# TensorE multiplies a constant mask by the identity in three waits of a sort

## The chip, the cores and the metric

The kernel runs on one core of one Trainium2 chip. The metric is the device time of one execution in microseconds. The kernel before takes 1694.79 us, the median of 3 runs from 1694.64 to 1695.75.

## What is computed

A hybrid block over 2 x 1024 rows of 512 values: sliding window attention, a mixture of experts, a Mamba-2 mixer, and the same mixture of experts again, each with a layer norm ahead of it and a residual added. The change touches the two mixtures of experts:

```python
    x = x + _L0_attn_a_ref(_layernorm(x, axis=-1), L0_attn_a_w_qkv, L0_attn_a_w_out)
    x = x + _L0_ffn_ref(_layernorm(x, axis=-1), L0_ffn_gate_w, L0_ffn_w1, L0_ffn_w2)
    x = x + _L0_attn_b_ref(_layernorm(x, axis=-1), ...)
    x = x + _L0_ffn_ref(_layernorm(x, axis=-1), L0_ffn_gate_w, L0_ffn_w1, L0_ffn_w2)

        # _L0_ffn_ref
        logits = jnp.einsum('th,eh->te', x, gate_w)
        probs = jax.nn.softmax(logits, axis=-1)
        topw, sel = jax.lax.top_k(probs, TOP_K)
        topw = topw / jnp.sum(topw, axis=-1, keepdims=True)
        combine = jnp.zeros((T, E), dtype=x.dtype).at[jnp.arange(T)[:, None], sel].add(topw)
        gate_up = jnp.einsum('th,eoh->eto', x, w1)
        g, u = jnp.split(gate_up, 2, axis=-1)
        act = jax.nn.silu(g) * u
        expert_out = jnp.einsum('eti,ehi->eth', act, w2)
        out = jnp.einsum('eth,te->th', expert_out, combine)
```

There are 8 experts, each row goes to 2 of them, and an expert has 352 inner values.

## The kernel before

The program is four stages one behind the other: `attention`, `experts` with the tag moe_a, `mamba`, `experts` with the tag moe_b. Each stage is a block with a program for each engine, written out by hand with semaphores; between stages all engines meet at a barrier.

The kernel does not compute all experts for all rows. It sorts the (row, expert) pairs by expert into 39 slots of 128 rows, gathers the rows of a slot by an indirect DMA, multiplies them by the weights of the slot's expert, and adds the results to the rows in memory by an indirect DMA. The weights of three experts fit into a ring in SBUF (`load_expert`, L912, 4352 KB an expert, issued by SyncE); the first expert's load is issued as the block begins.

`run_slots` (L1033) holds the block. Its first part is the sort, one for each mixture of experts, and the engines take turns in it:

- VectorE (`sort_rows`, L1173) chooses the experts of the last two tiles (the first fourteen are chosen during the stage before) and raises `both_ready` (L975).
- TensorE (`rank_last`, L1298 to L1310) waits for it and counts, in 17 small bf16 matmuls into bank 3, the rank of each row in its expert (first L1302).
- VectorE makes the start of each expert, each row's place, and from them, in four parts, two tables of 8 x 39 values each (L1202, L1204, L1206); each part raises `tables_ready`. Then it computes the owner of each slot (L1208, L1210).
- TensorE (`lists`, L1312 to L1320) waits for each part and makes 64 fp32 matmuls into bank 7, each with its own 128 columns of weights and 78 columns streamed (L1317): they bring each row's number and weight to its slot.
- VectorE waits for all of them, makes the indices (L1212, L1213) and the tables of which ring place and which load a slot needs (`slots_ready`).
- GpSimd gathers the rows of slots 0, 1, 2 and 3 (L1084); the gather of slot 2 and on waits for rows turned.
- TensorE waits for `slots_ready`, reads four values into registers (L1277, L1280), waits for the gather, and turns the rows of slot 0 by four transposes (`turn`, L1244) into bank 0. ScalarE and VectorE split them in a high and a rest part (L1110, L1164). TensorE then makes the up products (`up`, L1261), 24 matmuls for slot 0 in two halves of 12, each streaming 352 columns in fp32r, and turns slot 1.

Behind that runs the steady part, slot by slot: up products, the turn of the activations (L1272), the turn of the next rows, and down products (`down`, L1292, 9 matmuls of 512 columns, into banks 6 and 7 by turns). The down products of slot 0 are the first ones to write bank 6, with `start` set in the first matmul. The reads of registers for slot s+2 stand behind the first and the second pass of three down products of slot s.

The operands of the change are constants: `identb` (L137), the 128 x 128 identity in bf16, and `ssd_mask` (L142), 128 x 512 in bf16, zeros and -1e30, made before the first stage. In `mamba`, `running_sums` (L2092) multiplies the same two, twice in a call, as the start of an accumulation. Matmuls in a row: each weight load (PEld in the profile) overlaps the matmul ahead of it.

Of the kernel before, what the change touches and what calls it, by code (L numbers as in the profile page):

```python
# [97 lines left out]
def spread(ap, axis, n):  # L98

    v = ap.unsqueeze(axis)  # L100
    shape = list(v.shape)
    shape[axis] = n
    return v.broadcast_to(shape)
# [929 lines left out]
def run_slots(core, tag, sem, x_rows, xn_rows, index, weight, place, needed, ends, w_split, weights_in, in_w, at, sort):  # L1033

    nc, bank, arena = core.nc, core.bank, core.arena
# [25 lines left out]
    with nc.Block(no_gpsimd_drain=True) as block:  # L1061
# [176 lines left out]
        def _(pe):  # L1238
# [59 lines left out]
            def rank_last():  # L1298
                E, N = EXPERTS, sort.EARLY
                pe.wait_ge(both_ready, 1)  # L1300
                out = rank_bank[:, 0:3 * E]
                nc.tensor.matmul(out, core.before[:], sort.both[:, N:N + 3].rearrange("p t e -> p (t e)"),  # L1302
                                 start=True, stop=False)
                for t in range(N):
                    nc.tensor.matmul(out.rearrange("p (t e) -> p t e", e=E), core.onesb[:],
                                     spread(sort.both[:, t], 1, 3), start=False, stop=False)
                nc.tensor.matmul(rank_bank[:, E:3 * E].rearrange("p (t e) -> p t e", e=E), core.onesb[:],
                                 spread(sort.both[:, N], 1, 2), start=False, stop=False)
                nc.tensor.matmul(rank_bank[:, 2 * E:3 * E], core.onesb[:], sort.both[:, N + 1], start=False, stop=True)\
                    .then_inc(ranks_made, 1)  # L1310

            def lists():  # L1312
                n = TOPK * TILES
                for j in range(n):
                    if j % PART == 0:
                        pe.wait_ge(tables_ready, j // PART + 1)
                    last = nc.tensor.matmul(list_bank[:, 0:2 * SLOTS].rearrange("p (c s) -> p c s", c=2),  # L1317
                                            sort.at_spot[:, j // TILES, j % TILES], sort.by_slot[:, :, j],
                                            start=(j == 0), stop=(j == n - 1))
                last.then_inc(lists_made, 1)  # L1320

            rank_last()
            lists()
            places, needs = {}, {}

            def look_up(s, j):
# [965 lines left out]
```

## Time and profile before

| | us |
|---|---|
| median of 3 runs | 1694.79 |
| the profiled execution, its own time | 1690.24 |
| its span, first to last instruction | 1688.4 |
| TensorE busy (matmul) | 1516.6 |
| VectorE busy | 906.7 |
| ScalarE busy | 715.7 |
| GpSimd busy | 604.4 |
| mean granted TensorE clock, share of full | 0.957 |

All rows come from one execution taken by the hardware profiler. Times of day count from the first instruction. PE is TensorE's matmul, PEld its weight load, DVE VectorE, ACT ScalarE, POOL GpSimd, SP SyncE. A matmul's duration is longer than its distance to the next one in a row, since they are pipelined; the end of a group is the end of its last one. The granted clock is 1.00 at 2.4 GHz and 0.50 at 1.2 GHz.

### The profile page before, as it was taken

Reading aid. Unit: us, or ns where it says so; the run is one execution under the profiler, and the core shown is the slowest. Engines: PE = TensorE matmul, PEld = TensorE weight load, DVE = VectorE, ACT = ScalarE, POOL = GpSimd, SP = SyncE. Lnnn points to the kernel's source line nnn. Section 1 sums busy time; section 2 is a strip of 40 time slices with the busy share of each in tenths; the row PEclk is TensorE's granted clock in tenths of the full one; section 3 lists DMA queues with packets and bytes.
Section 4 is the critical chain, followed back from the end, with each engine's and each line's share of the span. In section 5 each row is a group of like instructions: output and inputs, shape, how many; then the busy total and the mean of one; then the engine's idle time right before and its main releaser. Section 6 shows DMA issues by size and latency. Waiting matters only on the chain. (4 is left out here: it accounts for less than half of the span.)

```text
span 1688.4 us, 33729 instructions
## 1 busy us (share of the span) xinstructions
PE 1516.6 (90%) x11806; PEld 1249.9 (74%) x11822; DVE 906.7 (54%) x2087; ACT 715.7 (42%) x1776; POOL 604.4 (36%) x469
## 2 busy tenths in 40 slices
PE   3999999998689999995899999999999868999997
PEld 3787887786578888985767677666776447888897
DVE  3676677776622224225687785877857652222222
ACT  2666666666122224322554455544445302222232
POOL 5564555555122334433232223322223302333342
PEclk9999999999689999997999999999999968999999
DMA  5264454454559777533010101101000136787643
GB/s 207 88 207 145 173 199 158 165 188 169 184 188 337 195 228 208 117 62 90 14 33 20 51 20 33 32 20 47 24 20 20 32 125 207 232 238 223 186 88 57
DMA packets 94476, 212.34 MB, mean 126 GB/s; under 512 B 7184, under 2 KB 7184, under 8 KB 92944
## 3 DMA queue, kind: packets, MB, share of 16 engines
q1 hardware_dynamic: 76736, 166.58, 28.2%
q0 software_dynamic: 17472, 40.90, 12.1%
q10 hardware_dynamic: 144, 3.15, 0.5%
q8 instruction: 85, 1.39, 0.3%
q14 instruction: 39, 0.32, 0.1%
HBM read 136.94 MB, written 73.66 MB: 125 GB/s over the span
## 5 line engine op out<-in xcount | busy, mean ns | idle before, releaser
L1261 PE MATMUL bank<-ring,halves 128*128 x1872 | 336.2, 329 | 3.5 <-ACT halves L1110 3.5
L1261 PEld LDWEIGHTS bank<-ring,halves 128*128 128x128 f32 x1872 | 307.0, 191 | 11.2 <-issue 4.8
L498 POOL TENSOR_TENSOR arena<-arena 128x1024 f32<-128x1024 f32 x64 | 123.9, 1936 | 146.6 <-DVE arena L574 145.0
L1655 DVE SCALAR_TENSOR_TENSOR arena<-arena 128x256 f32<-128x256 f32 x240 | 146.1, 651 | 18.6 <-ACT arena L1857 15.8
L1120 ACT ACTIVATE arena<-bank 128x512 f32<-128x512 f32 x78 | 46.7, 598 | 221.1 <-DMA out_dram<-arena 79.9
L700 ACT ACTIVATE arena<-arena 128x256 f32<-128x256 f32 x256 | 126.4, 500 | 1.1 <-DVE arena L566 1.1
L779 PE MATMUL bank<-arena 128*128 128x128 f32 x1024 | 124.9, 281 | 1.7 <-ACT arena L681 0.8
L1084 POOL DMA_INDIRECT arena<-normalised_rows,arena x78 | 80.3, 1030 | 125.1 <-DVE arena L1213 56.9
L779 PEld LDWEIGHTS bank<-arena 128*128 128x128 f32 x1024 | 118.9, 195 | 7.6 <-issue 2.6
L1546 POOL TENSOR_TENSOR arena<-arena 128x1024 f32<-128x1024 f32 x16 | 31.3, 1959 | 249.3 <-ACT arena L1908 227.9
L2107 PE MATMUL bank<-arena 128*128 128x512 f32 x256 | 117.0, 611 | 1.2 <-ACT arena L1901 1.2
L1092 POOL DMA_INDIRECT mid_rows<-arena x39 | 61.8, 1586 | 155.7 <-issue 107.9
L1092 POOL DMA_INDIRECT out_dram<-arena x39 | 61.8, 1585 | 152.2 <-issue 106.3
L1110 ACT ACTIVATE halves<-bank 128x512 fp32r<-128x512 f32 x78 | 46.7, 598 | 158.1 <-PE bank L1244 155.5
L1159 DVE TENSOR_TENSOR moe_b_act_rest<-bank,moe_b_act_high 128x384 fp32r<-128x384 f32 x39 | 21.8, 558 | 154.1 <-ACT moe_b_act_high L1125 149.9
L2022 PE MATMUL bank<-halves,w_in_high 128*128 128x256 f32 x640 | 94.8, 292 | 5.7 <-ACT arena L1857 4.3
L2107 PEld LDWEIGHTS bank<-arena 128*128 128x128 f32 x256 | 48.5, 194 | 68.7 <-issue 67.1
L1159 DVE TENSOR_TENSOR moe_a_act_rest<-bank,moe_a_act_high 128x384 fp32r<-128x384 f32 x39 | 21.7, 557 | 126.6 <-ACT moe_a_act_high L1125 126.6
L2022 PEld LDWEIGHTS bank<-halves,w_in_high 128*128 128x128 f32 x640 | 83.6, 194 | 7.4 <-ACT arena L1857 4.5
L1865 ACT ACTIVATE arena<-arena 128x256 f32<-128x256 f32 x80 | 35.6, 500 | 110.2 <-DVE arena L1655 110.1
L1164 DVE TENSOR_TENSOR halves<-bank,halves 128x512 fp32r<-128x512 f32 x78 | 53.9, 691 | 52.0 <-ACT halves L1110 52.0
L819 PE MATMUL bank<-ident,arena 128*128 128x128 f32 x512 | 70.0, 282 | 7.0 <-POOL arena L498 7.0
(263 smaller groups left out, 3184.0 us busy)
## 6 DMA issues: line engine op xcount, KB each, us to landing
ring<-expert_halves SPq DMA_DIRECT2D x16, 4352.0 KB
expert_halves<-expert_high SPq DMA_DIRECT2D x16, 1088.0 KB, 8.5
expert_halves<-expert_rest SPq DMA_DIRECT2D x16, 1088.0 KB, 10.7
arena<-in_w_dram SPq DMA_DIRECT2D x8, 1088.0 KB, 6.5
normalised_rows<-arena SPq DMA_DIRECT2D x33, 256.0 KB, 2.0
arena<-in_x_dram SPq DMA_DIRECT2D x32, 256.0 KB, 2.8
arena<-mid_rows SPq DMA_DIRECT2D x32, 256.0 KB, 2.8
w_in_raw<-in_in_w_dram SPq DMA_DIRECT2D x16, 290.0 KB
```

The source lines that it names most:

```text
L498: nc.gpsimd.tensor_tensor(held, held, spread(rinv[:, HG * g:HG * g + HG], 2, 2 * P), ALU.mult)\
L700: last = nc.scalar.activation(held, held, ACT.Exp, scale=-1.0, bias=nmax[:, h:h + 1], accum_out=psum_p[:, h:h + 1])
L779: last = nc.tensor.matmul(proj[:, c * P:c * P + P], wqkv[:, k, first + c * P:first + c * P + P], xnT[:, k], start=(k == 0), stop=(k == KD ...
L819: last = nc.tensor.transpose(b[:, j * P:j * P + P], probs[:, g // 2, HG * (g % 2) + 2 * half + j // 2, (j % 2) * P:(j % 2 + 1) * P], core. ...
L1084: nc.gpsimd.indirect_dma_start(out=rows[:, s % 2], out_offset=None, in_=xn_rows, in_offset=bass.IndirectOffsetOnAxis(ap=index[:, s:s + 1], ...
L1092: nc.gpsimd.indirect_dma_start(out=x_rows, out_offset=bass.IndirectOffsetOnAxis(ap=index[:, s:s + 1], axis=0), in_=y[:, s % 2], in_offset= ...
L1110: nc.scalar.activation(rows_parts[0][:, par], bank[0][:], ACT.Copy).then_inc(rows_high, 1)
L1164: nc.vector.tensor_tensor(rows_parts[1][:, par], bank[0][:], rows_parts[0][:, par], ALU.subtract)\
L1261: last = nc.tensor.matmul(bank[1 + 2 * par + part][:, 0:INTER], rows_parts[a][:, par, k * P:k * P + P], weights(at, b, (2 * k + part) * IN ...
L1655: last = nc.vector.scalar_tensor_tensor(out=slot[:, j], in0=cin[:, c, k:k + PAIR], scalar=taps[:, c, k:k + 1], in1=slot[:, j], op0=ALU.mul ...
L2022: last = nc.tensor.matmul(unit_banks[unit][:, j * PAIR:(j + 1) * PAIR], w_parts[b][:, k, at:at + P], x_parts[a][:, k], start=((a, b, k) == ...
L2107: last = nc.tensor.matmul(bank[7][:], yT[:, k], w_out[:, k], start=(k == 0), stop=(k == KY - 1))
```

## The change

A helper on TensorE makes n matmuls of the identity by the mask, each of 512 columns, into bank 6, each with `start` and `stop` set, so that it overwrites what stands there. It is called three times in each sort: with 3 ahead of the ranks, with 16 between the ranks and the lists, with 18 between the lists and the wait for `slots_ready`. Nothing reads the results, no semaphore is added, and nothing else is changed.

```diff
@@ -1319,8 +1319,17 @@
                 last.then_inc(lists_made, 1)
 
+            def stay_busy(n):
+
+                for _ in range(n):
+                    nc.tensor.matmul(bank[6][:], core.identb[:], core.ssd_mask[:].rearrange("p a b -> p (a b)"),
+                                     start=True, stop=True)
+
+            stay_busy(3)
             rank_last()
+            stay_busy(16)
             lists()
+            stay_busy(18)
             places, needs = {}, {}
```

## Rows read from the trace of the kernel before

**Rows 1.** The page: span, and granted clock in 40 slices, in tenths.

```profile
span 1688.4 us, 33729 instructions
...
PEclk9999999999689999997999999999999968999999
```

**Rows 2.** TensorE's waits in the first sort: total us, times, longest.

```profile
PE bank L1317 <- DVE arena L1206: 6.0, 1, 6.0
PE bank L1244 <- DMA arena<-normalised_rows,arena: 5.2, 1, 5.2
```

**Rows 3.** Windows: length, busy us of PE PEld DVE ACT POOL, clock, DMA share, GB/s.

```profile
449.30:455.20 5.90, 0.00 (x0) 0.00 (x0) 5.29 (x21) 0.00 (x0) 0.00 (x0) 0.50 1.04 394
...
462.50:465.90 3.40, 3.40 (x18) 3.40 (x17) 0.00 (x0) 0.00 (x0) 0.00 (x0) 0.50 0.00 0
...
471.50:474.30 2.80, 0.00 (x0) 0.00 (x0) 0.05 (x1) 0.00 (x0) 1.49 (x2) 0.50 0.42 108
...
476.30:479.50 3.20, 3.11 (x11) 3.11 (x12) 0.56 (x1) 0.00 (x0) 0.92 (x1) 0.50 0.29 82
479.70:482.40 2.70, 2.69 (x18) 2.44 (x17) 0.00 (x0) 0.00 (x0) 0.00 (x0) 1.00 0.00 0
```

**Rows 4.** Timeline, first sort: start us, us, what, count, idle before and releaser.

```profile
447.27 0.24 DVE L965 MAX8 arena<-logits 128x8 f32<-128x8 f32 x2 [1.11 <-PEq L118]
...
448.68 0.20 PE L1302 MATMUL bank<-arena,before 128*128 128x24 bf16 x1 [2.79 <-DVE arena L975]
...
455.29 13.73 PEld L1317 LDWEIGHTS bank<-arena 128*128 128x128 f32 x64 [6.08 <-DVE arena L1206]
455.29 13.94 PE L1317 MATMUL bank<-arena 128*128 128x78 f32 x64 [6.00 <-DVE arena L1206]
...
459.54 0.44 DVE L1210 TENSOR_REDUCE arena<-arena 128x39 f32<-128x273 f32 x1
...
474.38 1.12 PE L1244 MATMUL bank<-ident,arena 128*128 128x128 f32 x4 [5.15 <-DMA arena<-normalised_rows,arena]
...
476.39 5.57 PE L1261 MATMUL bank<-ring,halves 128*128 x24 [0.89 <-ACT halves L1110]
```

**Rows 5.** Timeline, second sort.

```profile
1381.67 13.94 PE L1317 MATMUL bank<-arena 128*128 128x78 f32 x64 [5.99 <-DVE arena L1206]
...
1402.61 6.57 PE L1261 MATMUL bank<-ring,halves 128*128 x24 [0.89 <-ACT halves L1110]
```

**Rows 6.** Timeline, the same kinds of work at full clock; the second row at half.

```profile
1351.34 0.97 PEld L230 LDWEIGHTS bank<-gate,arena 128*128 128x128 f32 x8 [0.92 <-ACT arena L224]
...
1370.38 1.71 PEld L230 LDWEIGHTS bank<-gate,arena 128*128 128x128 f32 x8 [0.92 <-ACT arena L224]
...
481.80 0.60 PE L1244 MATMUL bank<-ident,arena 128*128 128x128 f32 x4
...
492.62 2.17 PE L1261 MATMUL bank<-ring,halves 128*128 x12
```

**Rows 7.** Instructions of L2092, and of L844 from 435: ns min/median/max, first to last start.

```profile
L2092 PE MATMUL bank<-ssd_mask,identb x16: 377/379/379, 811.8 to 1329.8; 128*128 128x512 bf16 x16
...
L844 PE MATMUL bank<-wo_high,halves x7: 632/632/767, 435.4 to 438.1; 128*128 128x512 f32 x7
```

**Rows 8.** Windows in moe_a, two where TensorE waits, and what follows the first.

```profile
544.46:547.87 3.41, 1.41 (x8) 1.04 (x9) 1.13 (x3) 1.93 (x4) 1.59 (x1) 1.00 1.04 404
547.87:551.30 3.43, 3.43 (x10) 2.66 (x11) 0.61 (x1) 0.00 (x0) 0.99 (x1) 0.50 1.10 338
...
609.30:612.70 3.40, 1.67 (x12) 1.38 (x11) 0.00 (x0) 0.51 (x2) 0.00 (x0) 1.00 0.41 123
```

**Rows 9.** Reads of registers on TensorE's queue, and a down product.

```profile
L1277 PEldq TENSOR_LOAD <-arena x1: 302/302/302, 500.5 to 500.5; - x1
...
L1280 PEldq TENSOR_LOAD <-arena x2: 298/302/305, 471.6 to 472.9; - x2
...
501.71 1.66 PE L1292 MATMUL bank<-ring,moe_a_act_high 128*128 x6
```

## Prediction

> **What bounds the kernel now.** I read the page first: 1688.4 us of span, and a row of granted clock that stands at nine tenths nearly everywhere, with dips in two regions, around the eleventh and the thirty-third of the forty slices [rows 1]. These are the two places where a block of experts begins with its sort. The waits of TensorE there come next: it waits 6.0 us for VectorE's tables and 5.2 us for the gather of the first rows [rows 2]. The windows give the clock of each stretch: 0.50 in the wait for the tables, 0.50 in the middle of the list matmuls although TensorE is busy for all 3.40 us of 3.40, 0.50 in the wait for the gather, 0.50 in the first 3.2 us of the up products, and 1.00 only behind them [rows 3]. So in the sort TensorE works at 1.2 GHz, and the reader is to see that the 64 list matmuls do not lift the clock by themselves, though they run for 13.94 us on end [rows 4], while the up products do.
>
> The timeline gives the chain, which is the same in both sorts. VectorE starts at 447.27, TensorE has the ranks done at 455.29 - 6.00 = 449.29, VectorE makes tables, the list matmuls run from 455.29 to 469.23, VectorE turns them into indices, GpSimd issues the gather, it lands, TensorE turns the rows from 474.38 for 1.12 us, ScalarE copies, and the up products of the first slot run from 476.39 for 5.57 us [rows 4]. VectorE has nothing to do from about 460.0 (its last operation of the sort starts at 459.54 and takes 0.44) until the lists are done [rows 4]. So TensorE is the bound in the lists, the turn and the up products, and each microsecond there ends the program a microsecond earlier, as the experts behind the sort are started by these products; the loads of their weights are started by the rows turned and move along.
>
> **The change, part by part.** It removes nothing and moves nothing. It adds 3 + 16 + 18 matmuls of 512 bf16 columns per sort, 37 in each, 74 in all, that write a bank which the first down product starts afresh. They add no wait on a semaphore; what stands behind them on TensorE is the work that they precede.
>
> *Price of one.* The same operation, identity by mask, is in the mamba stage, where its matmul takes 379 ns [rows 7]. In a row the distance counts, not the duration: 512 columns at 2.4 GHz are 0.213 us, at 1.2 GHz 0.427 us. The trace doesn't show a row of bf16 ones; the nearest, 512 columns of fp32r at 0.50, has 7 starts between 435.4 and 438.1, 0.45 apart [rows 7]. I take 0.427 and keep 0.45 as the upper end.
>
> *First wait, 3 of them.* If TensorE enters the block with VectorE at 447.27, 3 x 0.427 = 1.28 plus about 0.1 for the first weight load (an estimate from the start) ends at 448.65, and the ranks start at 448.68 [rows 4]. Nothing to 0.15 late; I take 0.05.
>
> *Second wait, 16 of them.* They start at 449.29 and the lists may start at 455.29, so there are 6.00 us. All at 1.2 GHz they take 6.83, 0.83 too long. In the first sort dense products lift the clock 3.3 us after their start (476.39 to some point after 479.5) [rows 3, 4]; in the second they take 6.57 us instead of 5.57 [rows 5], so it came later: at full clock 12 of them take 2.17 [rows 6], 0.168 apart with 0.32 for the last (an estimate), at 1.2 GHz 352 columns make 0.293, and 6.57 us are then 19 of 23 distances at half rate, 5.6 us. If the clock rises x us after the start, the filler ends x + (6.83 - x)/2 after it: 5.07 for 3.3, 6.2 for 5.6. Nothing late in the one and 0.2 in the other; between the ends 0 and 0.83 I take 0.1, since the dense products are the nearest rows.
>
> *Lists at full clock.* Their distance is set by the weight load of 128 fp32 columns, since a load with hardly any columns behind it has the same: 8 loads before 8-column matmuls take 0.97 us at full clock and 1.71 where the clock has fallen [rows 6]. That is 0.121 and 0.214 for one, and the 64 loads of the lists in 13.73 us make 0.215 [rows 4]. At full clock a list matmul takes between half of that, 0.107, and 0.121, which has the long end of the last load in it; 64 take 6.9 to 7.7, I take 7.3: 6.6 less. VectorE keeps up: all four tables are done before 459.54 [rows 4], one every 1.3 us, and TensorE would take one in 16 x 0.11 = 1.8.
>
> *Third wait, 18 of them.* At full clock 18 x 0.213 = 3.84 us in a wait of 5.15 (469.23 to 474.38) [rows 4]: nothing, 1.3 us are left. At half rate 7.69: 2.5 late. Behind them stand four reads of registers which take 2.7 us from the moment when the slots are ready, so they must not wait for the filler: the last starts at 472.9 [rows 9]. In the steady loop such a read is made at 500.5, though in the code it stands behind the first three down products, which start at 501.71 [rows 9], so they run beside the filler. If they had to wait for its end they would be over 3.84 + 2.7 = 6.5 after the lists, 1.4 too late in each sort; I take 0.
>
> *Turn and up products.* Four transposes 1.12 to 0.60: 0.52 less [rows 4, 6]. 12 up products take 2.17 at full clock [rows 6], so 24 take 4.2 (the second dozen follows without a start of its own), against 5.57 and 6.57 [rows 4, 5]: 1.4 and 2.4 less.
>
> *Sum.* First sort: -6.6 - 0.52 - 1.4 + 0.05 + 0.1 = -8.37. Second: -9.37. Together -17.7 us. Nothing takes the cover away: the load of the first expert's weights runs beside the tables (no transfers in the window at 462.5) [rows 3], so a gather some 7 us earlier meets no traffic.
>
> A sentence of the Trainium skill speaks against the change: TensorE: Matmul & The Clock Gate, Why this matters for your kernels, says that keeping TensorE busy without a break brings it to the full clock. By that, lists of 13.94 busy us should run at full clock already and filling the waits would give at most the turn and the up products, some 5 us. The row says otherwise, 0.50 all along [rows 3], so I go by the row.
>
> **The rivals.** *Held only in part.* Once high, the clock must survive stretches that are half full: the gap that a quick filler leaves before the lists (0 to 0.9 us), the lists themselves (78 columns per 128 loaded), and the 1.3 us, turn and 0.9 us between the last filler and the up products. The trace shows both outcomes: a stretch of 3.4 us with TensorE busy for 1.67 kept 1.00, one with 1.41 busy was followed by 0.50 [rows 8]. The lists are busy throughout, so I think that they hold it; the last gap is the weak one. Falling there leaves 6.6 + 0.52 - 0.15 = 6.97 of one sort's gain; losing it in both gives -13.9, in one -15.3 or -16.3. If it falls inside the lists, about half of them are quick (3.3 us), the last filler is partly slow (about 1 late) and turn and up are quick: about -4.2 and -5.2 per sort, -9.4 for both and -13 or so for one.
>
> *Not counted, slower.* The filler multiplies an identity, nearly all zeros, by a mask of zeros and one large value, and no row here shows that such matmuls lift a clock; the only ones of the kind, pairs in mamba, stand in a stretch at full clock. If they don't count, every one costs 0.427: 0.1 + 0.83 + 2.54 = 3.5 per sort, +7.0. It turns slower from the point where the last filler, at 18 x the distance, exceeds 5.15 us, a distance of 0.286, with nothing won in the lists. Against it: the array streams 512 columns whatever they hold.
>
> The Trainium skill (TensorE: Matmul & The Clock Gate, Part 4: PE-mode transpose) says that transposes don't count as busy the way matmuls do; the filler has the identity as an operand, but isn't issued as a transpose, and if the rule reached it the time would be that of this rival.
>
> *It does not do what it says.* If only the up products profit (clock rising late, lists slow): -0.52 - 1.4 and -0.52 - 2.4, plus 0.83 and about 1 in each sort for late fillers: -1.2, which can't be told from no change.
>
> **How the numbers follow.** The profiled execution took 1690.24 us for its span of 1688.4; the median shown is 1694.79, 4.55 above. Taking 17.7 off gives 1672.5 for a profiled execution and 1677.1 for the median, which I predict. Its own range is -16 to -19.5. Chances: this 0.70; held in part 0.22 (-9 to -16.5); only turn and up 0.02; not counted 0.06 (+7.0, 1701.8). The range for 8 in 10 takes the forecast and most of the second: 1674.5 to 1683. What a measurement of this kernel can tell from no change is about 0.2%, 3.4 us. Faster by more: 0.92; within: 0.02; slower by more: 0.06.
>
> **What would show it.** In the changed profile the window over the lists reads 1.00 and they take 7.2 to 7.5 us; the wait before them is nearly gone; the turn takes 0.60; the 24 up products 4.0 to 4.3. Lists at 13.9 us with the filler 0.427 apart would show the slower rival; up products at 5.6 or more behind quick lists the gap after the last filler. A turn that starts more than 5.2 us after the lists would show that the fillers or the reads behind them are late. And if all of this is as written and the end is not 17 to 18 us earlier, something behind the sort, a transfer, took it back.

## Result

| | us |
|---|---|
| before, median of 4 runs (1694.64 to 1696.12) | 1695.27 |
| after, median of 4 runs (1677.29 to 1681.86) | 1679.55 |
| profiled execution: before / after | 1690.24 / 1681.86 |
| span: before / after | 1688.4 / 1680.1 |
| mean granted clock: before / after | 0.957 / 0.967 |

The ratio is 0.9907, 95% interval 0.9889 to 0.9925: 15.7 us quicker by the medians, where 17.7 were forecast. The two profiled executions differ by only 8.4 us; the stages below show where the rest lies in this pair.

The page of the changed kernel, lines that answer to [rows 1]; each dip at a sort was two slices at 6 and 8 tenths and is one at 7:

```profile
span 1680.1 us, 33893 instructions
...
PEclk9999999999799999997999999999999979999999
```

The windows of the changed kernel's first sort, which answer to [rows 3] (length, busy us of PE, PEld, DVE, ACT, POOL, clock, DMA share, GB/s):

```profile
449.40:452.40 3.00, 3.00 (x12) 1.07 (x9) 2.53 (x12) 0.00 (x0) 0.00 (x0) 0.50 0.98 382
452.50:454.40 1.90, 1.90 (x9) 0.69 (x7) 1.69 (x7) 0.00 (x0) 0.00 (x0) 1.00 1.05 396
454.60:455.40 0.80, 0.00 (x0) 0.00 (x0) 0.80 (x3) 0.00 (x0) 0.00 (x0) 1.00 1.06 392
455.60:459.00 3.40, 3.40 (x32) 3.40 (x32) 3.30 (x9) 0.00 (x0) 0.00 (x0) 1.00 1.06 390
...
466.10:469.50 3.40, 1.29 (x7) 0.52 (x5) 0.18 (x1) 0.60 (x1) 0.86 (x2) 1.00 0.56 154
469.60:472.90 3.30, 3.30 (x11) 3.30 (x12) 0.41 (x1) 0.00 (x0) 0.77 (x1) 0.50 0.29 79
```

The filler starts at half clock and has brought the full one about 3.1 us later; an idle gap of 0.99 us follows, the clock stays; in the lists TensorE is at 32 matmuls in 3.40 us where [rows 3] had 18. The last two windows are the gap behind the last filler: the clock is still 1.00 in it and 0.50 when the up products come. TensorE's timeline of both sorts, which answers to [rows 4] and [rows 5]:

```profile
447.46 1.44 PE L1325 MATMUL bank<-ssd_mask,identb 128*128 128x512 bf16 x3 [1.38 <-PEq L118]
448.87 0.20 PE L1302 MATMUL bank<-arena,before 128*128 128x24 bf16 x1
...
449.35 5.13 PE L1325 MATMUL bank<-ssd_mask,identb 128*128 128x512 bf16 x16
455.48 7.37 PE L1317 MATMUL bank<-arena 128*128 128x78 f32 x64 [0.99 <-DVE arena L1206]
462.68 4.05 PE L1325 MATMUL bank<-ssd_mask,identb 128*128 128x512 bf16 x18
468.00 0.66 PE L1244 MATMUL bank<-ident,arena 128*128 128x128 f32 x4 [1.27 <-DMA arena<-normalised_rows,arena]
469.55 5.63 PE L1261 MATMUL bank<-ring,halves 128*128 x24 [0.89 <-ACT halves L1110]
...
1374.82 4.91 PE L1325 MATMUL bank<-ssd_mask,identb 128*128 128x512 bf16 x16
1380.95 7.37 PE L1317 MATMUL bank<-arena 128*128 128x78 f32 x64 [1.23 <-DVE arena L1206]
1388.16 4.05 PE L1325 MATMUL bank<-ssd_mask,identb 128*128 128x512 bf16 x18
1393.28 0.66 PE L1244 MATMUL bank<-ident,arena 128*128 128x128 f32 x4 [1.08 <-DMA arena<-normalised_rows,arena]
1394.83 4.11 PE L1261 MATMUL bank<-ring,halves 128*128 x24 [0.89 <-ACT halves L1110]
```

In both sorts the lists take 7.37 us instead of 13.94 and nothing starts late. In the second the up products take 4.11 instead of 6.57; in the first they stay at 5.63 (before 5.57).

The profiled executions in six stretches, from the starts of the instructions named (of the up products that of their first weight load):

| from - to | before | after | difference |
|---|---|---|---|
| start - ranks of the first sort | 448.68 | 448.87 | +0.19 |
| ranks - up products of slot 1, first sort | 34.59 | 27.62 | -6.97 |
| to the last scatter of moe_a | 278.61 | 278.04 | -0.57 |
| mamba with the ends of the stages around it, to the ranks | 613.18 | 619.81 | +6.63 |
| ranks - up products of slot 1, second sort | 35.42 | 25.91 | -9.51 |
| to the last scatter of moe_b | 272.49 | 274.39 | +1.90 |

The two sorts bring 16.5 us. Mamba, in which not one instruction is changed, takes 6.6 us longer. That takes back two fifths of the 16.5 in this pair, and it is the first question to the experiments.

### The profile page after: what moved, and what is told of

It is laid out like the page before. It is cut to its first block and busy times, and to the rows that moved or that the text cites. A ratio compares the mean times of both kernels' runs of the same rounds, so it can differ in the third digit from the quotient of the medians.

```text
span 1680.1 us, 33893 instructions
## 1 busy us (share of the span) xinstructions
PE 1529.3 (91%) x11896; PEld 1246.7 (74%) x11896; DVE 908.3 (54%) x2087; ACT 716.3 (43%) x1776; POOL 601.9 (36%) x469
## 3 DMA queue, kind: packets, MB, share of 16 engines
q10 hardware_dynamic: 144, 3.15, 0.5%
```

## Experiments

"Ranks to up" is in all tables the time from the first rank matmul to the up products of slot 1 (before 34.59 and 35.42, after 27.62 and 25.91); "mamba" is the time from its first normalised tile to the ranks of the second sort (before 602.51, after 609.15). A version with one run has no interval.

### Delay alone ahead of mamba, and a second profile of the kernel before

At the end of moe_a's block, on VectorE, five memsets in the kernel before, one in the changed kernel (the line that declares the semaphore `padded` is left out):

```diff
+            if in_w is not None:
+                dve.wait_ge(added, 16 * SLOTS)
+                pad = Chain(dve, padded)
+                for _ in range(5):          # 1 in the changed kernel
+                    pad(nc.vector.memset(bank[5][:], 0.0))
```

> The kernel before with VectorE making five memsets of a free bank, one behind the other, at the end of the first experts' block, about 2.7 us of pure delay ahead of mamba. In the changed kernel mamba came 7.3 us earlier and took 6.6 us longer than before (from its start to the ranks of the second sort), and the clock fell for a short stretch in more of its turns. Theory (where mamba lies against the moments at which the clock is set decides which weak stretches lose it, and nothing else): a delay alone changes mamba's length too, by some us, with the clock falling at other turns than in the kernel before; a value of 3 to 6 us longer if it lands where the changed kernel does. Rival (the fillers themselves lengthen mamba, by something that lasts): mamba as long as before within 0.3 us and the clock falling at the same turns, total +2.7.

> The changed kernel with one such memset at the same place, about 0.6 us of delay. Theory: mamba's length moves again, by more than the delay; if it lands where the kernel before does, mamba is 5 to 6 us shorter than in the changed kernel's profile and the whole is 4 to 6 us quicker than that profile in spite of the delay. Rival (lasting effect of the fillers): mamba stays 6.6 us longer than before, total +0.6.

> The kernel before once more, for a second profile. Theory (mamba's length moves with the turns in which the clock falls, in the kernel before as well): mamba takes 604 to 610 us instead of 602.5 if the clock falls in more than the five turns of the first profile, and the stretches of the two sorts are the same (34.6 and 35.4 from the ranks to the up products of slot 1, the second one between 34.0 and 36.0). Rival (602.5 is what mamba takes in the kernel before, and the change lengthens it by 6 us): 602.5 within 0.5.

| | ranks to up | mamba | the whole, median |
|---|---|---|---|
| before, 5 memsets | 34.61, 35.36 | 607.20 | 1697.70 (10 runs), ratio 1.0019 [1.0002, 1.0037] |
| changed, 1 memset | 27.68, 25.83 | 608.81 | 1681.38 (6 runs), ratio 0.9919 [0.9893, 0.9944] |
| before, again | 34.52, 35.40 | 607.68 | 1691.51 (1 run) |

With five memsets and no filler in the kernel, mamba is 4.7 us longer than in the first profile of the kernel before; but the second profile of that kernel, unchanged, has it 5.2 us longer too. So no effect of the delay on mamba is shown, and the median with the delay, 3.4 us above the 1694.30 timed beside it, is little more than the memsets themselves (3.15 us from the first to the end of the last). The rival in its full size (the fillers lengthen mamba by 6.6 us) falls by the second profile. A small part of it doesn't: the three profiles without fillers have 602.5, 607.2 and 607.7, the eleven with fillers 607.3 to 612.1, 609.3 on average, so that 1 to 3 us that the change gives back in mamba stay possible. The windows of the second profile of the kernel before, over three stretches early in mamba's loop at half clock, and below them the same times of day in its first profile (mamba starts 2.9 us later there, so the work in them isn't quite the same; from 801.0 to 1083.7 us that profile is at 1.00 throughout):

```profile
871.30:874.70 3.40, 3.40 (x16) 3.24 (x15) 1.49 (x4) 1.99 (x5) 0.00 (x0) 0.54 0.00 0
...
943.00:946.30 3.30, 3.30 (x16) 3.16 (x15) 1.31 (x2) 1.75 (x5) 0.00 (x0) 0.53 0.00 0
1014.70:1018.00 3.30, 3.30 (x16) 3.22 (x15) 1.18 (x2) 1.61 (x5) 0.00 (x0) 0.54 0.00 0
```

```profile
871.30:874.70 3.40, 3.40 (x34) 3.31 (x34) 1.61 (x4) 2.73 (x6) 0.00 (x0) 1.00 0.00 0
943.00:946.30 3.30, 3.30 (x25) 3.05 (x24) 1.30 (x2) 2.68 (x7) 0.00 (x0) 1.00 0.00 0
1014.70:1018.00 3.30, 3.23 (x17) 2.40 (x16) 2.50 (x7) 2.78 (x7) 0.35 (x1) 1.00 0.03 5
```

In the 3.3 us ahead of each of the three TensorE is busy for 2.76, 2.71 and 2.71 us; such a stretch is called weak here. The second profile has eight short stretches at half clock in mamba's loop, the first one five. Three more and 5.2 us more make 1.7 us for each. The first profile of the kernel before, on which the forecast was worked out, had the shortest mamba of all 14 profiles. It doesn't explain why that execution lay 4.55 us under its median: the second one, with a mamba 5.2 us longer, took 1691.51 us, only 1.3 more, since its other stages were shorter, and lay 2.5 under the median timed beside it.

What was expected of the one memset was wrong: it did not bring the changed kernel's mamba back to 602.5; it took 608.8, the length that the rival had given. The falls follow each other 71.7 us apart in mamba's loop, save the last one, and the same part of the loop loses the clock in some executions and not in others. What decides it, and whether its place in time can move it, was not shown.

### One group of fillers at a time

```diff
 e_only16                e_no16                 e_no3
-stay_busy(3)            stay_busy(3)          -stay_busy(3)
 rank_last()             rank_last()            rank_last()
 stay_busy(16)          -stay_busy(16)          stay_busy(16)
 lists()                 lists()                lists()
-stay_busy(18)           stay_busy(18)          stay_busy(18)
```

> The changed kernel with only the 16 matmuls between the ranks and the lists; those ahead of the ranks and those behind the lists are left out. Theory (the clock is what the lists lack, and the 16 bring it): lists about 7.4 us in both sorts as in the changed kernel, but in the wait behind them the clock falls, so the turn takes 1.1 us and the 24 up products 5.6 to 6.6: 6.5 us gained per sort, 13 at the two places against the kernel before. Rival (the three groups work only together, the clock falls in the lists): lists at 13.9 us or between, nothing gained.

> The changed kernel without the 16; the 3 and the 18 stay. Theory: lists at half clock, 13.9 us; the 18 behind them start slow, need 3.3 to 5.6 us to bring the clock and end 5.5 to 6.6 us after the lists, so the turn comes 0.3 to 1.5 us later than before after the lists' end, but turn (0.6) and up products (4.1) are quick: gain of 0.5 to 2.5 us per sort. Rival (matmuls of the mask don't count, something else quickened the lists): the 18 take 7.7 us and the turn comes 2.5 late, up products slow.

> The changed kernel without the 3 matmuls ahead of the ranks. Theory (the 3 only fill; the 16 are enough since they need 3.3 us or a bit more of dense work): lists in 7.4 us in both sorts, ranks up to 0.1 us earlier, the 16 up to 0.5 us longer than the 4.9 to 5.1 they took. Rival (the 3 are needed to bring the clock in time): the 16 take over 6.2 us and the lists start late, or part of them runs at half clock.

| | lists | lists' end to turn | up products x24 | ranks to up |
|---|---|---|---|---|
| only the 16 | 7.37, 7.37 | 5.19, 4.97 | 5.50, 6.48 | 27.99, 28.74 |
| without the 16 | 13.94, 13.94 | 5.61, 5.25 | 4.10, 4.10 | 33.06, 32.69 |
| without the 3 | 7.37, 7.37 | 5.12, 5.00 | 5.61, 4.11 | 27.57, 25.98 |

TensorE's timeline, first sort with only the 16 (one record of the fillers is missing), then without them:

```profile
456.61 7.37 PE L1317 MATMUL bank<-arena 128*128 128x78 f32 x64 [0.91 <-DVE arena L1206]
469.17 1.12 PE L1244 MATMUL bank<-ident,arena 128*128 128x128 f32 x4 [5.19 <-DMA arena<-normalised_rows,arena]
471.17 5.50 PE L1261 MATMUL bank<-ring,halves 128*128 x24 [0.89 <-ACT halves L1110]
```

```profile
455.94 13.94 PE L1317 MATMUL bank<-arena 128*128 128x78 f32 x64 [5.99 <-DVE arena L1206]
470.10 5.56 PE L1325 MATMUL bank<-ssd_mask,identb 128*128 128x512 bf16 x17 [0.22 <-issue]
475.49 0.60 PE L1244 MATMUL bank<-ident,arena 128*128 128x128 f32 x4
```

The parts are nearly as expected (without the 16, the turn of the second sort comes 5.25 us after the lists instead of 5.5 or more, and the gain there is 2.7 us instead of at most 2.5). The 16 bring 6.6 and 6.7 us, nearly all of it in the lists. The 18 keep the clock over the wait for the gather: 0.4 of 7.0 us in the first sort, where the clock is lost a moment later anyway, and 2.8 of 9.5 in the second. Without the 16, the 18 (with the 3) bring 1.5 and 2.7 us, although they start at half clock and the turn comes 0.3 to 0.5 us late. The 3 bring nothing: ranks to up is 27.57 and 25.98 without them, 27.62 and 25.91 with them. The single run without them took 1674.3 us, which looked like a further gain of 5 us; so it was timed again.

> The changed kernel without the 3 once more, timed. Theory (the 3 bring nothing and carry the risk of the early rise): lists of 7.4 us in both sorts again, the median of the whole within 2 us of the change's, on either side, as the dips in mamba decide. Rival (the 1674.3 of the single run show a gain of 5 us from leaving the 3 away): a median of 1673 to 1676.

Median 1680.85 (4 runs), ratio 0.9918 [0.9898, 0.9938], lists 7.37 in both sorts, ranks to up 27.64 and 25.80. The 1674.3 came from short stretches elsewhere (mamba 607.6, experts of moe_b 270.7; in the second 612.1 and 274.3).

### What is streamed

```diff
-                for _ in range(n):
-                    nc.tensor.matmul(bank[6][:], core.identb[:], core.ssd_mask[:].rearrange("p a b -> p (a b)"),
-                                     start=True, stop=True)
+                for _ in range(2 * n):
+                    nc.tensor.transpose(bank[6][:, 0:P], core.ones[:], core.ident[:])
```

> The changed kernel with each of the fillers replaced by two transposes of 128 x 128 fp32 (ones against the identity), so 6, 32 and 36 of them; each is 0.213 us at half clock and 0.109 at full, as in the turn of the rows, so the time filled is the same. Theory (what keeps the clock up is that the array is streamed through, by what operation does not matter): lists in 7.4 us, as in the changed kernel. Rival (transposes don't count for the clock): lists at 13.9 us, the last 36 take 7.7 us, the turn comes 2.5 us late, and the kernel is some 6 us slower than before.

First sort: lists 7.37, ranks to up 27.69. These transposes do for the clock what the mask does there. The profile lists them as MATMUL of 128 x 128 fp32, as it does the turns of rows, and doesn't say in which mode the engine ran them. The second sort was not as expected:

```profile
1368.94 4.41 PE L1325 MATMUL bank<-ident,ones 128*128 128x128 f32 x32
1375.08 11.97 PE L1317 MATMUL bank<-arena 128*128 128x78 f32 x64 [1.72 <-DVE arena L1206]
1386.84 6.09 PE L1325 MATMUL bank<-ident,ones 128*128 128x128 f32 x36
1393.27 0.65 PE L1244 MATMUL bank<-ident,arena 128*128 128x128 f32 x4 [0.33 <-issue]
```

The 32 ended after 4.41 us instead of 5.2, left 1.72 us idle, and the lists took 11.97. The next experiment had the same.

### Bridging the last gap

```diff
             lists()
-            stay_busy(18)
+            stay_busy(23)
...
             turn(0)
+            stay_busy(4)
             pe.wait_ge(weights_in, needs[0])
```

> The changed kernel with 23 matmuls behind the lists instead of 18 and 4 more between the turn of slot 0's rows and the up products. Theory (in the first sort the clock falls in the gap between the last filler and the up products, and only there): the clock stays at 1.00 there, the 24 up products take 4.1 instead of 5.6 us in the first sort, the second sort is as in the changed kernel; the turn comes 5.2 us after the lists and the up products 1.54 us after it, or at most 0.2 later. From the ranks to the up products of slot 1: 26.1 in the first sort (changed kernel 27.6), 25.9 in the second; 1.5 us quicker in all, hardly more than the noise of the whole. Rival (the clock falls at a set place of the program whatever fills the gap): 5.6 us again and the total unchanged or later by what the 9 matmuls cost.

Beside it the changed kernel once more:

> The changed kernel once more, beside the version with the bridged gap. Theory: the same stretches in both sorts within 0.1 us (27.6 us from the ranks to the up products of slot 1 in the first sort), while mamba and the experts behind the sorts differ by some us from the profile seen, because the clock falls in other turns. Rival (mamba's 609 us are a fixed consequence of the change): 609.1 within 0.3 us.

| | lists | up products x24, first sort | ranks to up | mamba | the whole, median |
|---|---|---|---|---|---|
| bridged | 7.37, 12.01 | 4.12 | 26.11, 32.25 | 608.36 | 1678.03 (5 runs), 0.9900 [0.9882, 0.9918] |
| change again | 7.37, 7.37 | 5.66 | 27.73, 25.97 | 608.92 | 1679.81 (4 runs), 0.9921 [0.9906, 0.9937] |

The expectation for the change again was in part wrong: the sorts repeat within about 0.1 us, but mamba did not move by some us. It took 608.92, within the 0.3 that the rival gave around 609.15. So the changed kernel has 609.15 and 608.92, and 608.81 with the memset, and the 1 to 3 us from above stay open.

In the first sort the bridge does what it should: the gap is filled, the clock holds, and the 24 up products take 4.12 us. So the fall there is made by the thin stretch from the last filler to the up products. In the second sort the clock fell in the lists. Windows of the bridged version: the gap before the lists, the first 2.2 us of the lists, the rest, the filler behind them:

```profile
1377.20:1378.90 1.70, 0.00 (x0) 0.00 (x0) 1.60 (x6) 0.00 (x0) 0.00 (x0) 1.00 1.04 394
1379.00:1381.20 2.20, 2.20 (x20) 2.20 (x20) 2.13 (x6) 0.00 (x0) 0.00 (x0) 0.98 1.05 392
1381.30:1390.70 9.40, 9.40 (x46) 9.40 (x46) 2.27 (x6) 0.00 (x0) 0.00 (x0) 0.50 0.31 115
1390.80:1394.80 4.00, 4.00 (x11) 1.48 (x10) 1.88 (x10) 0.00 (x0) 2.04 (x2) 0.50 0.14 17
```

There the 16 had taken 4.31 us, since the clock came early, and 1.81 us stayed idle. Two explanations offered themselves: such a gap makes the clock fall a little later, in the lists, or the fall is chance. The 3 fillers ahead of the ranks can be the reason for the early clock, since they begin the dense work 2 us sooner. Two more runs, 12 instead of 16 in the changed kernel, and the bridged version without the 3:

```diff
 e_12                    e_no3_bridge
 stay_busy(3)           -stay_busy(3)
 rank_last()             rank_last()
-stay_busy(16)           stay_busy(16)
+stay_busy(12)           lists()
 lists()                 stay_busy(23)   # and 4 behind turn(0)
```

> The changed kernel with 12 fillers ahead of the lists instead of 16, the 3 and the 18 as they are. Theory (an idle gap of nearly 2 us or more before the lists, with the lists behind it, makes the clock fall): the 12 end 4.0 to 4.4 us after their start, the gap is 1.7 to 2.1 us, and in at least one of the sorts the clock falls in the lists, which then take 9 to 12.5 us. Rival (the lists hold any clock that they are given at their start): 7.4 us in both sorts, the gap is harmless.

> No filler ahead of the ranks, 16 ahead of the lists, 23 behind them, 4 between the turn and the up products. Theory (with the 3, the clock can rise early, the 16 then end 1.7 us or more before the lists, and the clock falls in the lists, as in the second sort of the version with the bridged gap and of that with transposes; without the 3 it can't rise before about 3 us of the 16 are done): lists 7.4 us in both sorts, the gap before them under 1.3 us, the up products of slot 0 in 4.1 us in both, from the ranks to the up products of slot 1 26.0 to 26.1 and 25.8 to 26.0. In all 1.5 us quicker than the change and the best of all versions, if only by the noise. Rival (the early fall in the lists was chance and the 3 have nothing to do with it): lists of 12 us may come up again in one of the sorts.

With 12 the lists took 13.73 and 13.94 us, as if there were no filler, more than the 9 to 12.5 expected. Windows of the gap and of the lists in both sorts:

```profile
451.90:454.20 2.30, 0.39 (x3) 0.09 (x1) 2.13 (x8) 0.00 (x0) 0.00 (x0) 1.00 1.05 395
454.30:467.50 13.20, 13.20 (x64) 13.20 (x64) 4.36 (x11) 0.00 (x0) 0.00 (x0) 0.50 0.40 146
1384.20:1386.00 1.80, 0.01 (x1) 0.00 (x0) 1.66 (x6) 0.00 (x0) 0.00 (x0) 1.00 1.04 390
1386.40:1400.00 13.60, 13.60 (x64) 13.60 (x65) 4.46 (x11) 0.00 (x0) 0.00 (x0) 0.50 0.40 147
```

The clock is 1.00 while TensorE is idle and 0.50 once it works. In a longer wait it falls within the wait: with only the 16, behind the lists of the first sort, TensorE is idle from 463.98 to 469.17, and the clock is 1.00 in 464.10:467.40 and 0.50 in 467.50:469.10. Gaps of 1.92 and 2.10 us made the lists slow here, 1.72 and 1.81 in the two versions above. All shorter ones were harmless, in the other sorts of all versions with 16 fillers, up to 1.51 in the second sort of the change again and 1.69 in that of the changed kernel with the memset. In this version only the filler was shortened, by the 4 that would have filled the gap, so the gap is the cause of its two falls. In the two versions above the same is likely, from four falls in four longer gaps and none below. A fixed limit isn't shown: 1.69 and 1.72 lie too near each other, and the fall came 2.2 us into the lists in those two versions and within 0.3 us of their start here, so where the gap lies in time may count as well as how long it is. The kernel took 1691.27 us (1 run).

Without the 3 and with the bridge: lists 7.37 in both, gaps of 1.00 and 1.20, up products 4.11 and 4.12, ranks to up 26.08 and 25.93. This is the best pair of sorts of all versions, 1.5 us better than the changed kernel's. The whole is 1678.67 (6 runs), ratio 0.9915 [0.9897, 0.9932], not to be told from the change's 0.9907 and 0.9921. That the 3 cause the early clock is likely and not shown: with them the 16 (or 32 transposes) took 5.13 to 5.26 us in the first sorts and 4.31 to 4.91 in the second ones, in the three profiles of versions without the 3 but with the 16 and something behind the lists they took 5.08 to 5.14 and 4.89 to 6.27. One pair of quick sorts can't rule out chance.

## Why the prediction was right

*The mechanism.* Each step of the chain but one is in the profile. The lists took 7.37 us against 7.3 forecast, where they had 13.94; their price came from [rows 6], weight loads with hardly a column behind them, and held. The distance of a filler is 0.216 us at full clock and 0.427 at half (0.213 and 0.427 taken). Second wait: 5.13 and 4.91 us of 6.1, so none late (0.1 taken); first wait: the ranks start 1.41 us after VectorE's first operation of the sort (448.87 and 447.46), as before (448.68 and 447.27) [rows 4], so nothing (0.05 taken). Third wait: 4.05 us in 5.15, and the reads of registers ran beside it: the last starts at 466.5, the last filler ends at 466.73. The bridged version shows it as well, where the turn of the second sort starts 6.7 us after the lists, with the filler's own end. Turn: 1.12 to 0.66 (0.60 forecast).

*The rule that spoke against it.* By the Trainium skill (TensorE: Matmul & The Clock Gate, Why this matters for your kernels), which has TensorE kept busy without a break to reach the full clock, busy lists would have been quick before. They were at 0.50 in the middle with TensorE busy for all of it [rows 3] and took 13.94 us, as they do again without the 16; with the 16 they begin at 1.00, hold it behind a short enough gap and take 7.37. The same page's sentence on transposes (Part 4: PE-mode transpose), which stood behind the slower rival, was not borne out by the fp32 transposes of this case: 32 of them lifted the clock as the mask did (5.21 and 4.41 us). The slower rival itself falls by the change: the 16 masks took 5.13 and 4.91 us, where it had 6.83.

*The term that was off.* Up products of the first sort, -1.4 forecast, +0.06 measured. It is the first of the rivals, the clock lost between the last filler and the up products, in one sort of two. That sort gained 6.97 us, the figure that the rival had given. It is no chance: all six profiles of the first sort with 18 masks or 36 transposes behind quick lists lost it there, the two bridged ones did not. The forecast named this gap as the weak one and still took it as held. Its own row for a fall, 1.41 busy of 3.41 [rows 8], is near what the first sort then had, 1.29 of 3.40; but the second sort had hardly more and kept the clock:

```profile
1391.50:1395.00 3.50, 1.53 (x9) 0.69 (x7) 0.39 (x1) 0.60 (x1) 0.93 (x2) 1.00 0.56 150
```

Why one sort loses it and the other never does, with idle gaps of 1.27 and 1.08 us ahead of the turn and 0.89 behind it in both, stays open.

*How far it was luck.* What came is not the case that the forecast called likeliest, with all gains kept (-17.7, its own range -16 to -19.5), but the rival for one sort lost, which had 0.22 with its kin and a sum of -16.3. The two are 1.4 us apart, less than the medians can tell, and the range of 1674.5 to 1683 took in both. That the time lies in it speaks for the lists (13 of the 17.7 us), not for the up products.

*The sum.* -17.7 forecast, -16.5 in the sorts, -15.7 by the medians of this comparison and -13.4 by those of the second. The 1 to 3 us between sorts and medians are within what mamba and the experts move by themselves (602.5 to 612.1 and 269.9 to 274.4 us over the profiles of all versions); whether the change gives back 1 to 3 us in mamba was not settled. The two profiles taken by themselves gave 8.4 and would have misled: the step from the profiled execution to the median, +4.55, was taken without asking in which stage it lay, and the runs don't say it either.

*The rival in the lists.* It did not come up in the changed kernel's two profiles, but in two near relatives, which gained 3.2 and 3.7 us in that sort where the rival had said 5.2: 4.6 us more in the lists, and the turn 1.3 and 1.8 us later. Its trigger was the gap, which I had put at 0.9 us at most, since I let the clock rise no earlier than 3.3 us after the start of the 16; with the 3 and the ranks ahead of them it can rise sooner.

## What to carry to other kernels

Where an engine waits and then runs work that is too thin to lift its own clock, filling the wait with matmuls that nobody reads is worth up to half the time of the work behind it, here 6.6 us for 16 matmuls. Fill up to the work: an idle rest of up to 1.69 us was harmless here, one of 1.72 cost 4.6 of the 6.6 us and one of 1.92 nearly all, so size the filler for its quickest run as well as for its slowest. And compare profiles stage by stage before explaining a total: an untouched stage differed here by 5.2 us between two executions of one and the same kernel, a third of the gain.

## What was not expected of the hardware

- Matmuls of 78 columns with a new fp32 weight load each keep TensorE busy by the profile and leave the granted clock at 0.50 for 13.94 us; started at 1.00 behind a gap of up to 1.69 us they hold it for 7.37 us.
- After an idle gap the clock can fall when the work is back: 1.00 in gaps of 1.72 to 2.10 us, 0.50 in the lists, from their start or 2.2 us later.
- Transposes of 128 x 128 fp32 lift the clock as matmuls of the mask do: 32 of them took 5.21 us in the first sort, and the lists behind them 7.37.
- In mamba a weak stretch costs 1.7 us when the clock falls behind it, and the kernel before has five such falls in its loop in one execution and eight in another.
